# Two of four batches routed inside the attention loop, one dealt there, and other PSUM banks for the shared experts

## The chip, the cores and the metric

The kernel runs on one core of a Trainium2 chip. The core has five engines with a queue each: TensorE (PE, its weight loads shown as PEld), VectorE (DVE), ScalarE (ACT), GpSimd (POOL) and SyncE (SP). An engine works its queue in order; a wait for a semaphore holds everything that stands behind it. SP and POOL also issue DMA transfers. The metric is the time of one execution in microseconds (us) on the device.

## The reference

Four batches of 256 rows with 256 columns go through gated cross attention with 32 heads, and then through a mixture of experts: two shared experts for all rows, and the best 6 of 32 routed experts for each row.

```python
x = x + tanh(g_xattn[0]) * xattn(layernorm(x), ctx, pos, pos, Wq, Wkv, Wout, bout)
flat = layernorm(x).reshape(-1, 256)                 # 1024 tokens
shared = sum(relu(flat @ sw1 + sb1) @ sw2 + sb2 for 2 shared experts) / 2
probs = softmax(flat @ router_w + router_b)          # 32 experts
topk_p, topk_i = top_k(probs, 6); gates = topk_p / sum(topk_p)
routed = sum(gates[:, e] * (relu(flat @ rw1[e] + rb1[e]) @ rw2[e] + rb2[e]) for e in topk_i)
x = x + tanh(g_ffn[0]) * (shared + routed)
```

## The kernel before

The order of the work is written out by hand, engine by engine; semaphores tie the queues together. A tile is 128 rows, a batch `b` has two tiles (`TB`), and there are `NT` = 8 tiles. The program has four stages.

**Projections and rotations** of all batches come first.

**Attention** runs over 32 steps `i` (`GROUPS`; 8 of them, `NG`, to a batch), each with four heads. In step `i` PE transposes queries and keys of step `i+2` into `T_BANK` (`transposes`), makes scores (`score`), waits for DVE's row maxima (`row_max`, L821), which POOL writes beside the queries (`maxima`, L414 and L416), makes shifted scores of earlier steps (`shifted_score`), and multiplies weights by values (`values`). ACT makes the exponentials (L549) and empties `T_BANK` (L506). In odd steps DVE also divides a finished pair of groups (`normalise`, L832 and L837). When a batch is done, its rows are transposed and projected in the same loop: `attention_transposed` at the end of steps 13, 21 and 29, and one tile's `output_projection` (L1286) at the end of steps 15, 17, 23, 25 and 31, all into `T_BANK`. The PE's next `transposes` waits until ACT or DVE (`residual`, L848) has read that bank.

**Routing and shared experts** follow the loop. For each batch: normalised rows (`normalised_rows`), their transposes, the router's scores, the best eight (`choose`), gates (`gates`), counts of earlier rows for each expert by matmul (`counts`), and from these the place of each row and choice (`places`, up to `slot`, L957). POOL then deals: 12 indirect DMAs per batch (L462), 48 in all, each sending a tile's rows to their places in `rows_by_block` in HBM. The shared experts (`shared_hidden`, `shared_transposed`, `shared_out`) stand between these steps on PE, tile by tile, in banks 0, 7, 1, 2, 4 and 6.

**Blocks.** SP waits for all 48 deals (`dealt`) and loads blocks of 128 rows (`xs`, L343); for each of 79 blocks PE works one routed expert (L1450 to L1477), and POOL adds the result to a sum in HBM (L470). PE's first block waits for the last `shared_sum` too:

```python
            pe.wait_ge(shared_ok, NT)
            pe.wait_ge(slot_ok, B)
```

Of the kernel before, what the change touches and what calls it, by code (L numbers as in the profile page):

```python
# [21 lines left out]
def gated_cross_attention_moe(  # L22
# [38 lines left out]
    SPARE = 208  # L61
# [4 lines left out]
    with ExitStack() as keep:  # L66
# [36 lines left out]
        ramp_c = sb("ramp_c", [P, NT])  # L103
        ramp_p = sb("ramp_p", [P, 1])
        gfh = sb("gfh", [P, 1])

        top8 = sb("top8", [P, NT, 8])
# [15 lines left out]
        def sa(name, shape, dt=F32):  # L123
# [33 lines left out]
        XROW_AT, XT_AT = TB * D, 3 * H * HR + TB * D  # L157
        xrow = v_flat[:, XROW_AT:XROW_AT + NT * ROW].rearrange("p (n c) -> p n c", c=ROW)
        xT32 = v_flat[:, XT_AT:XT_AT + KD * TOK].rearrange("p (k n) -> p k n", k=KD)
        assert XROW_AT + NT * ROW <= 3 * H * HR and XT_AT + KD * TOK <= 6 * H * HR  # L160
# [17 lines left out]
        lg = sb("lg", [P, NT, NE])  # L178
        chosen = [sb(f"chosen{i}", [P, TB, TOPK, NE], BF16) for i in range(2)]
        steps8 = sb("steps8", [P, NE, NT])  # L180
        placed = sb("placed", [P, TB, TOPK, NE])
# [39 lines left out]
            sem(n) for n in ("dif_ok", "ex_ok", "mask_ok", "masks_ok", "rk_mm", "row_ok", "slot_ok", "dealt"))  # L221
        later_ok, be_mm, be_ok, isbe_ok, b1_mm, b1_ok = (
# [14 lines left out]
        C_PJ = [[T_BANK, T_BANK] for b in range(B - 1)] + [[S_BANK[0], T_BANK]]  # L237
        C_XT, C_LG, C_RK = [banks[1], banks[2], banks[4], T_BANK], banks[3][:, 0:N], O_BANK[:, N:2 * N]
        C_UP, C_BE = O_BANK[:, 0:B * NE], O_BANK[:, P:P + NBP]
        C_B1 = [O_BANK[:, N + c * P:N + c * P + NBP] for c in range(2)]  # L240
        assert B * NE <= P and NT * NE <= N
        SH_BANK, SHT_BANK = [banks[0], banks[7]], banks[1:3]
        SO_BANK = [banks[4][:, 0:D], banks[6][:, 0:D]]
# [4 lines left out]
        PROJ_STEPS = {NG * (b + 1) + 7 + 2 * t: (b, t) for b in range(B - 1) for t in range(TB)}  # L248
# [110 lines left out]
        def _(pool):  # L359
            steps = [0]  # L360

# [57 lines left out]
            def constants(part):  # L419
# [6 lines left out]
                if part == 1:  # L426
                    pool.wait_ge(pv_mm, 2 * NG)
                    pool.iota(xrow[:, :, X_ID].bitcast(U32), pattern=[[P, NT]], base=0, channel_multiplier=1).then_inc(id_ok, 1)
                    pool.iota(ramp_e[:, :], pattern=[[1, NE]], base=0, channel_multiplier=0, allow_small_or_imprecise_dtypes=True)
                    pool.iota(ramp_c[:, :], pattern=[[P, NT]], base=0, channel_multiplier=0, allow_small_or_imprecise_dtypes=True)  # L430
                if part == 2:
                    pool.iota(ramp_b[:, :], pattern=[[1, NBP]], base=0, channel_multiplier=0, allow_small_or_imprecise_dtypes=True)
                    pool.iota(ramp_p[:, :], pattern=[[0, 1]], base=0, channel_multiplier=1,
                              allow_small_or_imprecise_dtypes=True).then_inc(ramps_ok, 1)

            for g in range(GROUPS):
                maxima(g)
# [14 lines left out]
            inverse_root(6, slice(3 * TB, NT))  # L452

            pool.wait_ge(blank_st, 16 * (SUMS + 1))
            pool.wait_ge(id_ok, 1)
            for b in range(B):
                pool.wait_ge(xn2_ok, TB * (b + 1))
                pool.wait_ge(row_ok, b + 1)
                pool.wait_ge(slot_ok, b + 1)
                for n in range(TB * b, TB * b + TB):  # L460
                    for k in range(TOPK):
                        pool.indirect_dma_start(xd, bass.IndirectOffsetOnAxis(ap=slot[:, n, k:k + 1], axis=0),  # L462
# [11 lines left out]
        def _(act):  # L474
# [109 lines left out]
            for i in range(GROUPS):  # L584
                step(i)
# [940 lines left out]
```

## Time and profile before

| | |
|---|---|
| time, median of 3 runs | 404.68 us (401.33 to 408.31) |
| the profiled execution's own time | 402.14 us |
| its span, first to last instruction | 400.4 us |
| TensorE's mean granted clock | 0.934 of full speed |
| PE, PEld busy | 336.3 us (84%), 263.7 us (66%) |
| DVE, ACT, POOL busy | 245.4, 213.8, 214.8 us |

Shares of the whole span are averages over stages with different limits, so the rows further below are of single stages. "Idle before" of an instruction names what ended the wait. The granted clock is 1.00 at 2.4 GHz and 0.50 at 1.2 GHz.

### The profile page before, as it was taken

The page shows a single profiled execution, that of the slowest core. Times are in us where ns is not written, and L with a number is a line of the kernel's source. Part 1 is how long each engine was busy: PE and PEld are TensorE (multiplying, and loading weights), DVE is VectorE, ACT ScalarE, POOL GpSimd, SP SyncE. Part 2 cuts the span into 40 slices and gives each one's busy share as a digit, 9 for nine tenths or more (in the row PEclk, how much of TensorE's full clock was granted, in tenths as well). Part 3 has the DMA queues.
Part 4 walks back from the last instruction along what each step waited for, and adds up shares of the span by engine and source line. Part 5 has one row for each costly group of instructions (what it writes and reads, how often), then busy time and mean ns, then how long its engine had stood idle before and what let it go on. Part 6 is the DMA issues. An engine that isn't in the chain of part 4 may idle for free.

```text
span 400.4 us, 8584 instructions
## 1 busy us (share of the span) xinstructions
PE 336.3 (84%) x2574; PEld 263.7 (66%) x2574; DVE 245.4 (61%) x765; ACT 213.8 (53%) x536; POOL 214.8 (54%) x242
## 2 busy tenths in 40 slices
PE   8789999999999997523667799999999999999900
PEld 5577666666666555422444589998999899989800
DVE  7997788788788868575440145554545454545526
ACT  4795899988988862110203255555555555555400
POOL 8465331101211112677777248788878887888840
PEclk9999999999999999666659999999999999999975
DMA  7799999983032041133333538888888888887589
GB/s 225 215 308 310 307 335 323 342 180 117 2 86 61 2 120 29 70 112 111 112 113 111 163 70 141 141 150 145 146 141 141 146 142 139 146 143 128 68 168 304
DMA packets 63295, 62.20 MB, mean 155 GB/s; under 512 B 6258, under 2 KB 61588, under 8 KB 63252
## 3 DMA queue, kind: packets, MB, share of 16 engines
q1 hardware_dynamic: 48532, 44.60, 38.3%
q0 software_dynamic: 13680, 17.05, 26.6%
q8 instruction: 24, 0.39, 0.4%
q10 hardware_dynamic: 1040, 0.01, 0.1%
q14 instruction: 19, 0.16, 0.1%
HBM read 29.01 MB, written 32.63 MB: 154 GB/s over the span
## 4 chain that ended last, share of the span: by engine, by line
PE 62%; DVE 14%; ACT 11%; DMA 6%; issue 4%; POOL 1%; SPq 0%; POOLq 0%; DVEq 0%; ACTq 0%
PE psum L1477 15%; PE psum L1459 11%; ACT probs L549 5%; PE psum L1186 5%; PE psum L1233 5%; DMA sum<-ob,xs 4%; PE psum L1395 4%; PE psum L1450 4%; PE psum L1468 4%; PE psum L1374 3%; DVE nmax L821 3%; PE psum L1204 2%; PE psum L1286 2%; PE psum L1087 2%; ACT Vx L631 1%
## 5 line engine op out<-in xcount | busy, mean ns | idle before, releaser
L470 POOL DMA_INDIRECT sum<-ob,xs x79 | 123.0, 1557 | 39.4 <-DVE ob L1057 34.5
L821 DVE TENSOR_REDUCE nmax<-psum 128x2 f32<-128x512 f32 x128 | 79.4, 683 | 10.4 <-PE psum L1186 9.7
L1477 PE MATMUL psum<-w,hT 88*128 (+1 forms) x316 | 81.5, 380 | 0.0
L549 ACT ACTIVATE probs<-psum 128x512 f32<-128x512 f32 x128 | 69.5, 597 | 12.5 <-PE psum L1204 11.4
L1057 DVE TENSOR_SCALAR ob<-psum,gate 128x256 f32<-128x256 f32 x79 | 38.2, 484 | 48.2 <-PE psum L1477 46.1
L668 ACT ACTIVATE hT<-psum,b1b 88x128 f32<-88x128 f32 x158 | 48.8, 358 | 35.2 <-PE psum L1468 35.2
L1459 PE MATMUL psum<-w,xT 128*128 x316 | 60.4, 314 | 0.3 <-ACT xT L659 0.3
L1477 PEld LDWEIGHTS psum<-w,hT 88*128 88x128 f32 (+1 forms) x316 | 53.8, 190 | 4.6 <-issue 0.3
L462 POOL DMA_INDIRECT rows_by_block<-Vx,slot x48 | 46.3, 966 | 18.0 <-issue 14.3
L414 POOL CAST Qx<-nmax 128x8 fp32r<-128x8 f32 x32 | 6.3, 197 | 84.0 <-DVE nmax L821 84.0
L659 ACT ACTIVATE xT<-psum 128x256 f32<-128x256 f32 x79 | 30.2, 383 | 38.9 <-PE psum L1450 38.9
L1459 PEld LDWEIGHTS psum<-w,xT 128*128 128x128 f32 x316 | 47.3, 190 | 1.0 <-issue 1.0
L1040 DVE COPY hb<-psum 128x176 f32<-128x176 f32 x79 | 27.0, 342 | 28.5 <-PE psum L1459 28.4
L1186 PE MATMUL psum<-QK 32*128 32x256 f32 x256 | 38.9, 319 | 3.3 <-DVE nmax L821 2.6
L1204 PE MATMUL psum<-QT,QK 32*128 32x256 f32 x256 | 37.7, 327 | 0.9 <-ACT probs L549 0.8
L1186 PEld LDWEIGHTS psum<-QK 32*128 32x128 f32 x256 | 25.8, 183 | 18.2 <-issue 10.5
L1233 PE MATMUL psum<-probs,Vx 128*32 128x256 f32 x512 | 34.3, 385 | 0.0
L1395 PE MATMUL psum<-w2s,Vx 128*128 128x256 f32 (+1 forms) x48 | 16.6, 495 | 19.4 <-ACT Vx L631 19.4
L1450 PE MATMUL psum<-ident,xs 128*128 128x128 f32 x158 | 30.1, 272 | 0.6 <-DVE x_sb L993 0.6
L1468 PE MATMUL psum<-ident,hb 128*88 128x128 f32 x158 | 30.2, 273 | 0.0
L1450 PEld LDWEIGHTS psum<-ident,xs 128*128 128x128 f32 x158 | 22.0, 140 | 8.8 <-DVE x_sb L993 1.0
L1204 PEld LDWEIGHTS psum<-QT,QK 32*128 32x128 f32 x256 | 25.1, 183 | 2.2 <-issue 1.1
(177 smaller groups left out, 476.4 us busy)
## 6 DMA issues: line engine op xcount, KB each, us to landing
rows_by_block<-blank SPq DMA_DIRECT2D x1, 10744.0 KB, 38.2
xs<-rows_by_block SPq DMA_DIRECT2D x79, 136.0 KB, 2.6
w<-in_L_ffn_rw_dram SPq DMA_DIRECT2D x2, 2816.0 KB, 21.3
w<-in_L_ffn_rw_dram SPq DMA_DIRECT2D x16, 352.0 KB
sum<-blank SPq DMA_DIRECT2D x3, 1152.0 KB, 13.5
w<-sum SPq DMA_DIRECT2D x12, 256.0 KB, 5.5
sum<-ob,xs POOLq DMA_INDIRECT x79, 4.0
x_sb<-in_x_dram SPq DMA_DIRECT2D x4, 256.0 KB, 4.0
```

Source lines behind the costliest of these rows:

```text
L462: pool.indirect_dma_start(xd, bass.IndirectOffsetOnAxis(ap=slot[:, n, k:k + 1], axis=0), xrow[:, n, :], None).then_inc(dealt, 16)
L470: pool.indirect_dma_start(yd[i], bass.IndirectOffsetOnAxis(ap=xs[b % ROWS_AHEAD][:, X_ID:X_ID + 1].bitcast(U32), axis=0), ob[i][:, :], Non ...
L549: act.activation(probs[g % 2][:, :, n, :], st_bank(g, n)[:, :].rearrange("p (t q) -> p t q", t=TB), ACT.Exp, scale=SCALE).then_inc(exp_ok, 1)
L668: ins = act.activation(hT[b % 2][0:HC, c, :], HT_BANK[b % 2][0:HC, c * P:(c + 1) * P], ACT.Relu, bias=b1b[0:HC, c, b:b + 1])
L821: dve.tensor_reduce(nmax[i % 2][:, :, n], S_BANK[(4 * i + n) % SB][:, :].rearrange("p (t k) -> p t k", t=TB), AX.X, ALU.max, negate=True). ...
L1186: ins = pe.matmul(S_BANK[(4 * i + n) % SB][:, qt * N:(qt + 1) * N], QK[i % RING][h, 0, qt * P:(qt + 1) * P], QK[i % RING][h, 1, :], start= ...
L1204: ins = pe.matmul(st_bank(i, n)[:, kt * N:(kt + 1) * N], QK[i % RING][h, 1, kt * P:(kt + 1) * P], QT[i % 2][h, :], start=True, stop=True)
L1233: ins = pe.matmul(O_BANK[HR * h:HR * h + HR, 0:N], Vx[:, TB * b + kt, GH * g + h, :], probs[i % 2][:, kt, h, :], start=(kt == 0 and not se ...
L1450: ins = pe.transpose(XT_BANK[b % 2][:, k * P:(k + 1) * P], xs[r][:, k * P:(k + 1) * P], ident[:, :])
L1459: ins = pe.matmul(H_BANK[b % 2][:, 0:HID], xT[b % 3][:, k, :], w1[:, k, bass.ds(expert[b] * HID, HID)], start=(k == 0), stop=(k == KD - 1))
L1468: ins = pe.transpose(HT_BANK[b % 2][0:HC, c * P:(c + 1) * P], hb[b % 2][:, c * HC:(c + 1) * HC], ident[:, :])
L1477: ins = pe.matmul(Y_BANK[b % 2][:, 0:D], hT[b % 2][0:rows, c, :], w2[0:rows, bass.ds(expert[b], 1), c, :].rearrange("p a n -> p (a n)"), s ...
```

## The change

Each step of the routing of batches 0 and 1 (`EARLY` = 2) moves into the attention loop, some steps after what it needs. For batch `b` they are: the inverse root and its refinement on POOL (`scales`, step 8b+16), normalised rows on DVE (8b+18), their transposes on PE (8b+19), the router's scores (8b+20), the choice on DVE and POOL (8b+21 to 8b+23), gates (8b+23). For batch 0 the counts follow (step 24), then the block numbers and places on POOL and DVE (25 to 27), and POOL issues seven of its deals after the maxima of steps 28 to 31. For batch 1 counts and `places` stand after the loop. Transposes, scores and counts use `T_BANK`. Output projections stand one step apart, at 14, 15, 22, 23, 30 and 31, so that the sixth, before behind the loop, is inside. Whole block counts come from rounding three times instead of from 256 comparisons and a sum. The shared experts get banks 2 and 3 (hidden), 4 and 1 (transposed) and 6 and 0 (result), and their first tiles stand ahead of the last batch's projection.

```diff
-        PROJ_STEPS = {NG * (b + 1) + 7 + 2 * t: (b, t) for b in range(B - 1) for t in range(TB)}
+        PROJ_STEPS = {NG * (b + 1) + 6 + t: (b, t) for b in range(B - 1) for t in range(TB)}
+        EARLY = B - 2
+        ROWS_STEPS = {NG * b + 19: b for b in range(EARLY)}
+        SCORE_STEPS = {NG * b + 20: b for b in range(EARLY)}
+        COUNT_STEPS = {24: 0}
...
-        SH_BANK, SHT_BANK = [banks[0], banks[7]], banks[1:3]
-        SO_BANK = [banks[4][:, 0:D], banks[6][:, 0:D]]
+        SH_BANK, SHT_BANK = banks[2:4], [banks[4], banks[1]]
+        SO_BANK = [banks[6][:, 0:D], banks[0][:, 0:D]]
...
+            EACH = TB * TOPK
+            DEALT_AT = {28: (0, 2), 29: (2, 3), 30: (3, 5), 31: (5, 7)}
             for g in range(GROUPS):
                 maxima(g)
...
+                if g in DEALT_AT:
+                    deal(*DEALT_AT[g])
+                for b in range(EARLY):
+                    if g == NG * b + 16:
+                        scales(b)
+                    if g == NG * b + 21:
+                        marks_of(b)
+                if g == 25:
+                    blocks_needed(0)
+                if g == 26:
+                    places_early(0)
+            deal(DEALT_AT[31][1], DEALT_AT[31][1] + 1)
+            inverse_root(EARLY + 4, slice(TB * EARLY, TB * EARLY + TB))
+            deal(DEALT_AT[31][1] + 1, EACH + EACH // 2)
             pool.wait_ge(pv_mm, GROUPS)
...
+            inverse_root(B + 3, slice(NT - TB, NT))
+            deal(EACH + EACH // 2, NT * TOPK)
...
                     pe.wait_ge(t_ok, i)
...
+                if i - AHEAD - 1 in ROWS_STEPS:
+                    pe.wait_ge(x2T_ok, ROWS_STEPS[i - AHEAD - 1] + 1)
+                if i - AHEAD - 1 in SCORE_STEPS:
+                    pe.wait_ge(lg_ok, SCORE_STEPS[i - AHEAD - 1] + 1)
+                if i - AHEAD - 1 in COUNT_STEPS:
+                    pe.wait_ge(rk_ok, COUNT_STEPS[i - AHEAD - 1] + 1)
...
-            second_rows_transposed(0)
+            second_rows_transposed(B - 2)
             outputs(PAIRS - 1)
-            second_rows_transposed(1)
-            router_scores(0)
-            router_scores(1)
+            router_scores(B - 2)
+            shared_hidden(0)
...
             attention_tile_transposed(B - 1, 1).then_inc(aT_mm, 1)
+            shared_hidden(1)
             for t in range(TB):
                 output_projection(B - 1, t)
```

On POOL, before, from the last `maxima` to the first deals (waits in brackets):

```order
L414 CAST Qx<-nmax1 128x2x4 [waits s_max]
L416 TENSOR_TENSOR Qx<-nmax1,Qx 128x2x4 [waits mhi_ok]
L378 TENSOR_TENSOR rough<-veps,halves 128x4 [waits var_ok]
L378 TENSOR_TENSOR rough<-veps,halves 128x2 [waits var_ok]
L448 MEMSET hT0 64x128 [waits root_ok,pv_mm]
L450 MEMSET Vx 32x128 [waits ones_ok]
L448 MEMSET hT1 64x128 [waits ones_ok]
...
L378 TENSOR_TENSOR rough<-veps,halves 128x2 [waits var_ok,ones_ok]
L462 DMA rows_by_block<-Vx,slot 10112x272 [waits row_ok,xn2_ok,slot_ok,id_ok,blank_st]
L462 DMA rows_by_block<-Vx,slot 10112x272 x11
```

And now, from the last `maxima`:

```order
L425 CAST Qx<-nmax1 128x2x4 [waits s_max]
L427 TENSOR_TENSOR Qx<-nmax1,Qx 128x2x4 [waits mhi_ok]
L502 DMA rows_by_block<-Vx,slot 10112x272 x3
L389 TENSOR_TENSOR rough<-veps,halves 128x2 [waits var_ok]
L502 DMA rows_by_block<-Vx,slot 10112x272 x4
L502 DMA rows_by_block<-Vx,slot 10112x272 [waits row_ok,xn2_ok,slot_ok,id_ok,blank_st]
L502 DMA rows_by_block<-Vx,slot 10112x272 x5
L534 MEMSET hT0 64x128 [waits root_ok,pv_mm]
L536 MEMSET Vx 32x128 [waits ones_ok]
...
L389 TENSOR_TENSOR rough<-veps,halves 128x2 [waits var_ok,ones_ok]
L502 DMA rows_by_block<-Vx,slot 10112x272 x6
```

Ahead of the last inverse root, which needs the last batch's variances, 18 deals now stand where none stood; 30 stand behind it.

On DVE, before, step 23 and the start of step 24 (the middle of attention):

```order
L832 RECIPROCAL rden0<-psum 128x16 [waits q2_ok,ot_mm,norm_ok]
L837 TENSOR_TENSOR attn<-psum,rden0 128x2x32 [waits rd_ok]
...
L821 TENSOR_REDUCE nmax1<-psum 128x2 [waits s_mm,m_ok]
L821 TENSOR_REDUCE nmax1<-psum 128x2 [waits s_mm] x3
L848 SCALAR_TENSOR_TENSOR x_sb<-psum,gx,x_sb 128x256 [waits pj_mm]
L821 TENSOR_REDUCE nmax0<-psum 128x2 [waits s_mm,m_ok]
```

And now, step 23 (`mask` and `red` belong to the routing of batch 0):

```order
L917 RECIPROCAL rden0<-psum 128x16 [waits q2_ok,ot_mm,norm_ok]
L922 TENSOR_TENSOR attn<-psum,rden0 128x2x32 [waits rd_ok]
...
L933 SCALAR_TENSOR_TENSOR x_sb<-psum,gx,x_sb 128x256 [waits pj_mm]
L906 TENSOR_REDUCE nmax1<-psum 128x2 [waits s_mm,m_ok]
L971 TENSOR_REDUCE mask<-Vx 128x64
L906 TENSOR_REDUCE nmax1<-psum 128x2 [waits s_mm] x2
L977 TENSOR_REDUCE red<-ex 128x2 [waits ex_ok]
L978 RECIPROCAL red<-red 128x2 [waits dve_step]
L979 SCALAR_TENSOR_TENSOR Vx<-ex,gf,red 128x2x6 [waits dve_step]
...
L813 BN_STATS stats<-x_sb 128x6 [waits pj_ok]
```

The residual that follows the even projection step 22 stands behind `normalise` in an odd step, and the routing's instructions stand among the maxima.

On PE, before, from the transposes of the last batch's attention to the first shared tile:

```order
L1263 MATMUL psum<-ident,attn 128x128 [waits exp_ok,norm0_ok,pj_ok]
...
L1286 MATMUL psum<-wout_sb,Vx 128x256 [waits aT_ok,out_w_ld]
...
L1335 MATMUL psum<-ident,Vx 128x128 [waits xn2_ok]
...
L1344 MATMUL psum<-rtw_sb,Vx 128x32 [waits lg_ok,x2T_ok]
...
L1364 MATMUL psum<-mask,before_ 128x32 [waits ramps_ok,o_ok,mask_ok]
...
L1374 MATMUL psum<-w1s,Vx 128x352 [waits pj_ok,ws_ld]
```

And now, from the end of attention to the last batch's projection:

```order
L1348 MATMUL psum<-probs1,Vx 32x256 x7
L1414 MATMUL psum<-ident,Vx 128x128 [waits masks_ok,xn2_ok]
...
L1359 MATMUL psum<-ident,oT1 128x128 [waits norm_ok,q2_ok,o_ok]
...
L1423 MATMUL psum<-rtw_sb,attn 128x32 [waits x2T_ok]
...
L1504 MATMUL psum<-w1s,attn 128x352 [waits exp_ok,ws_ld]
...
L1378 MATMUL psum<-ident,attn 128x128 [waits norm0_ok,pj_ok]
...
L1378 MATMUL psum<-ident,attn 128x128 [waits norm_ok]
...
L1504 MATMUL psum<-w1s,attn 128x352 x2
L1401 MATMUL psum<-wout_sb,Vx 128x256 [waits aT_ok,out_w_ld]
```

Two tiles of `shared_hidden` have moved ahead of the projection from which the last batch's variances come.

## Rows read from the trace of the kernel before

**Rows 1.** Windows by stage: busy us (instructions) per engine, granted clock, DMA share, GB/s.

```profile
100.00:130.00 30.00, 28.89 (x350) 19.01 (x349) 24.84 (x51) 26.22 (x57) 4.49 (x25) 1.00 0.19 50
...
170.00:176.00 6.00, 0.42 (x10) 0.31 (x8) 5.06 (x24) 0.00 (x0) 4.57 (x5) 0.78 0.31 116
```

**Rows 2.** Timeline, from the first deal to the first block: start, duration.

```profile
162.36 1.24 POOL L462 DMA_INDIRECT rows_by_block<-Vx,slot  x1 [3.67 <-DVE slot L957]
...
222.06 0.96 POOL L462 DMA_INDIRECT rows_by_block<-Vx,slot  x1 [0.30 <-issue]
...
224.50 20.77 SPq L343 DMA_DIRECT2D xs<-rows_by_block  x16
...
229.24 0.66 PE L1450 MATMUL psum<-ident,xs 128*128 128x128 f32 x4 [0.58 <-DVE x_sb L993]
```

**Rows 3.** DMA issues from 160 to 235 us: count, KB each, median us to landing.

```profile
xs<-rows_by_block SPq DMA_DIRECT2D x12, 136.0 KB, 3.0
rows_by_block<-Vx,slot POOLq DMA_INDIRECT x48, 2.4
```

**Rows 4.** Timeline of POOL, `maxima` of steps 10, 12, 13, 15 and 31.

```profile
66.19 0.20 POOL L414 CAST Qx<-nmax 128x8 fp32r<-128x8 f32 x1 [2.40 <-DVE nmax L821]
...
72.60 0.20 POOL L414 CAST Qx<-nmax 128x8 fp32r<-128x8 f32 x1 [2.40 <-DVE nmax L821]
...
76.13 0.20 POOL L414 CAST Qx<-nmax 128x8 fp32r<-128x8 f32 x1 [3.04 <-DVE nmax L821]
...
83.28 0.20 POOL L414 CAST Qx<-nmax 128x8 fp32r<-128x8 f32 x1 [3.17 <-DVE nmax L821]
...
140.28 0.20 POOL L414 CAST Qx<-nmax 128x8 fp32r<-128x8 f32 x1 [2.91 <-DVE nmax L821]
```

**Rows 5.** Timeline of attention, a projection step (23) and an odd step (25).

```profile
111.71 1.13 PE L1286 MATMUL psum<-wout_sb,Vx 128*128 128x256 f32 x4
...
116.38 0.26 DVE L832 RECIPROCAL rden<-psum 128x16 f32<-128x16 f32 x1 [0.18 <-ACT QT L555]
...
116.58 0.36 PE L1167 MATMUL psum<-ident_r,Qx 128*128 128x128 f32 x2
...
116.94 2.47 DVE L821 TENSOR_REDUCE nmax<-psum 128x2 f32<-128x512 f32 x4
...
117.68 0.38 PE L1186 MATMUL psum<-QK 32*128 32x256 f32 x1 [0.17 <-DVE nmax L821]
```

**Rows 6.** Groups of DVE instructions in routing: count, busy us, mean ns.

```profile
L911 DVE TENSOR_REDUCE mask<-chosen 128x64 bf16<-128x384 bf16 x4 | 3.2, 798 | 0.1
...
L908 DVE TENSOR_TENSOR chosen<-ramp_e,Vx 128x384 bf16<-128x384 f32 x4 | 2.3, 575 | 0.1
```

**Rows 7.** Timeline behind attention: roots, projection to variances, one `places`, shared tile 4.

```profile
150.25 0.70 POOL L378 TENSOR_TENSOR rough<-veps,halves 128x2 f32<-128x2 f32 x1 [6.39 <-DVE veps L736]
...
154.30 1.96 PE L1286 MATMUL psum<-wout_sb,Vx 128*128 128x256 f32 x8 [1.49 <-ACT Vx L609]
...
157.69 0.16 DVE L736 TENSOR_TENSOR veps<-mv,consts 128x2 f32<-128x2 f32 x1
...
170.46 0.43 DVE L933 TENSOR_TENSOR steps<-psum,ramp_c 128x256 f32<-128x256 f32 x1 [4.06 <-PE psum L1364]
...
175.07 0.18 DVE L971 TENSOR_TENSOR old_off<-old_off,off_up 128x32 f32<-128x32 f32 x1
...
216.11 1.56 PE L1395 MATMUL psum<-w2s,Vx 128*128 128x256 f32 x6 [0.99 <-ACT Vx L631]
```

**Rows 8.** Windows of 1 us, columns as in rows 1.

```profile
160.00:161.00 1.00, 0.00 (x0) 0.00 (x0) 0.91 (x3) 0.00 (x0) 0.00 (x0) 1.00 0.00 0
163.00:164.00 1.00, 0.58 (x3) 0.58 (x4) 0.97 (x9) 0.00 (x0) 0.70 (x2) 0.58 0.00 0
204.00:205.00 1.00, 0.61 (x4) 0.61 (x4) 0.29 (x2) 0.00 (x0) 0.70 (x2) 0.50 0.37 139
210.00:211.00 1.00, 1.00 (x4) 0.42 (x2) 0.00 (x0) 0.46 (x1) 0.69 (x2) 0.53 0.16 52
```

More of the change, by code:

```diff
@@ L177, in gated_cross_attention_moe @@
         ob = [sb(f"ob{i}", [P, D]) for i in range(SUMS)]
[L178 to L181, printed above, removed]
         upto_j = sb("upto_j", [P, P])
@@ new lines, in deal @@
+            def deal(first, last):
+                for j in range(first, last):
+                    n, k = j // TOPK, j % TOPK
+                    b = n // TB
+                    if k == 0 and n % TB == 0:
+                        pool.wait_ge(blank_st, 16 * (SUMS + 1))
+                        pool.wait_ge(id_ok, 1 + b // 2)
+                        pool.wait_ge(xn2_ok, TB * (b + 1))
+                        pool.wait_ge(row_ok, b + 1)
+                        pool.wait_ge(slot_ok, b + 1)
+                    pool.indirect_dma_start(xd, bass.IndirectOffsetOnAxis(ap=slot[:, n, k:k + 1], axis=0),
+                                            xrow[:, n, :], None).then_inc(dealt, 16)
@@ new lines, in block_ends, with slots, early @@
+            def block_ends(b, had):
+                return dve.tensor_tensor_scan(upto[:, b, :], had, consts[:, 0, 0:NE], upto[:, b - 1, NE - 1:NE] if b else 0.0,
+                                              ALU.add, ALU.add)
+            def slots(b):
+                with nc.allow_low_precision("whole numbers"):
+                    dve.tensor_reduce(slot[:, TB * b:TB * b + TB, :], placed[:, :, :, :], AX.X, ALU.add).then_inc(slot_ok, 1)
+            def early(i, part):
+                for b in range(EARLY):
+                    at = i - NG * b
+                    if (at, part) == (18, 0):
+                        dve.wait_ge(nstep_ok, b + 1)
+                        dve.wait_ge(pv_mm, NG)
+                        normalised_row(TB * b)
+                    if (at, part) == (18, 2):
+                        normalised_row(TB * b + 1)
+                    if (at, part) == (21, 0):
+                        scores(b)
+                    if (at, part) == (21, 1):
+                        then(eight_best(b))
+                    if (at, part) == (21, 2):
+                        where_best(b).then_inc(at8_ok, 1)
+                    if (at, part) == (22, 1):
+                        dve.wait_ge(exp_row_ok, b + 1)
+                        dve.wait_ge(pv_mm, 2 * NG)
+                        then(choice_of(b))
+                    if (at, part) == (23, 0):
+                        mask_of(b)
+                    if (at, part) == (23, 2):
+                        gate_sums(b)
+                if (i, part) == (26, 1):
+                    dve.wait_ge(had_ok, 1)
+                    block_ends(0, blocks[:, 0, :]).then_inc(upto_ok, 1)
+                if (i, part) == (27, 3):
+                    dve.wait_ge(placed_ok, 1)
+                    slots(0)
@@ L1433, in _ @@
             ins.then_inc(b1_mm, 1)
-            for n in range(2, NT):
+            for n in range(4, NT):
                 shared_out(n)
```

443 lines of the change are left out of this document (242 added, 201 removed).

## The prediction, made before the changed kernel had run

> **What bounds the kernel now.** I read the windows by stage first. In attention PE, ACT and DVE are all nearly full (28.89, 26.22 and 24.84 of 30 us) and POOL is nearly idle, 4.49 [rows 1]. Behind it the picture turns: from 170 to 176 us PE works 0.42 of 6 us while DVE (5.06) makes places and POOL (4.57) deals [rows 1]. So the stage between attention and the blocks is a chain, and the timeline tells which one ends last. POOL's 48 deals start at 162.36 and 222.06 us, 59.7 / 47 = 1.27 us apart; SP's loads go out at 224.50; PE's first block starts at 229.24, released by DVE's last shared sum [rows 2]. A deal lands 2.4 us and a block 3.0 us after its issue [rows 3], so the deals alone would have let the blocks start at 224.5 + 3.0 = 227.5. Two limits thus lie 1.7 us apart, the shared experts last and the dealing just behind. Removing work from one alone would give 1.7 us; this change moves both. From the first block to the end nothing is edited: that part keeps its length.
>
> I count from c, the start of the maxima of step 31, which is 140.28 [rows 4]. Before, the first deal is at c+22.1, the last at c+81.8, the first block at c+89.0.
>
> **What the change adds to attention.** A pair of steps in which `T_BANK` does no other work takes 72.60 - 66.19 = 6.41 us; with the attention transposes of step 13 it takes 83.28 - 76.13 = 7.15 [rows 4], so such a use costs 0.74. From step 13 to 31, 18 steps, it is 64.15 us, 6.46 over nine plain pairs, for seven uses: three transposes (2.2) and four projections, 1.06 each, about the 1.13 that PE spends on one [rows 5]. Now the same stretch holds thirteen uses.
> - Transposes of attention, three, 2.2, and of normalised rows, two: the same four transposes and one ACT copy, 1.5.
> - Projections at odd steps, two, 2.1.
> - Projections at even steps, three. The reader, DVE's residual, now stands behind `normalise` in an odd step. There PE's next transposes start at 116.58, but `normalise` ends at 116.94 [rows 5]; a residual behind it would hold PE until about 117.4. The score that follows, at 117.68, waits for the first maximum anyway [rows 5], so I charge 0.55 of these 0.84: 1.6 each, 4.8.
> - Router scores, two, at even steps. Their small matmuls I take at the projection's 1.06. Their reader stands behind the first maximum too (0.62 of L821's 2.47, and 0.2 more): PE is held until 117.8 and the score slips by 0.85 [rows 5]. 1.9 each, 3.8.
> - Counts, one: no row shows them beside attention. Between 0 and the 0.74 of a larger use, 0.4.
>
> Together 14.8, so 8.3 more than now. DVE adds the routing of two batches: the mask 0.80, the choice 0.58 [rows 6], and by the same group view some 2.6 for rows, scores, best eight and gates, 4.0 a batch. Mostly they fill the holes that the bank uses leave; where no use falls (steps 26 and 27 above all) DVE's maxima and `normalise` already fill 5.9 of 6.4. I charge 1.7 there. At step 29 a deal stands ahead of POOL's copy of the choice, for which DVE waits in step 30: 1.0 more. So attention ends **11 us later**. The bounds are 5 (all bank waits and DVE work hidden) and 17 (8.3 and all 8 us of DVE, none hidden).
>
> The other POOL work in attention (refinement, block numbers, places, seven deals) I cost at nothing: POOL has some 2.9 us free in every step, before each of these rows ("2.40", "3.17" [rows 4]), and no step gets more than about 2.8. A step that gets more delays the maxima by the excess.
>
> One rule speaks against dealing here. The deals before ran beside a DVE that worked 5.06 of 6 us, and kept to 1.27 us apart [rows 1, 2]. The Trainium skill (SBUF — State Buffer, "Who interferes with whom") says that DVE instructions with two SBUF inputs, or in a 2-port mode, and GpSimd's exclude each other for a whole instruction. By that each of seven deals could be held for one `chosen`, 0.58 us, 4 us in all and 395 for the sum; the trace shows no such lengthening.
>
> **What it takes out behind attention.** Now POOL, from c: maxima until c+0.5, three deals to c+4.6, an inverse root of 0.70 [rows 7], ten deals to c+18.0, four memsets to c+19.0. Then comes the root of the last batch, for which POOL waits, with 30 deals queued behind it. Before, that batch's projection starts at 154.30, c+14.0, and the variances are done 3.55 us later, c+17.6 [rows 7]. Now two hidden tiles stand ahead of the projection (each at most the 1.56 of a shared result [rows 7]) and one router less (1.0), which gives c+16.1; and `places(1)`, 4.8 us as one now takes [rows 7], stands ahead of the rows that PE transposes first. I walk it to c+16.5; at worst c+19. Variances at c+20.1, root at c+20.8, last of 30 deals at c+20.8+0.3+29 x 1.27 = c+57.9, landed at c+60.3, first block at **c+63.3** (62 to 66) against c+89.0.
>
> The slots are in time for that: batch 1's at c+8.2 for a deal at c+10.3, batch 2's by the same walk at c+27 for c+28, batch 3's at c+35 for c+44.
>
> The shared experts end earlier. Tile 4's result starts at 216.11 and the first block 13.1 us later [rows 2, 7]; by the walk tile 4 comes at c+41, so they would end at c+54, nine before the deals. **Dealing becomes the limit**, and PE idles for nine us. In the trace the granted clock falls from 1.00 to 0.50 after PE has idled from 159.9 to 163.4, and comes back only at 210.5 after it has worked from 204.4 on [rows 8]: 6.1 us at half speed, some 3.3 us of work late with the ramp. I charge the blocks 3.3 (0 to 3.5).
>
> **Sum.** c moves to 151.3, the first block to 214.6, and 3.3 are lost: 229.2 - 214.6 - 3.3 = 11.3 us gained. Against the profiled execution's 402.1 that is 390.8. The runs' median, 404.7, lies 0.6% above this execution, the lowest at 401.3; I take half of that and forecast 392.
>
> **The rivals.**
> - Attention hides nearly all (5 to 7 us longer) and the clock holds: 402.1 - (229.2 - 146.3 - 63.3) = 382.5 to 386. For it: DVE has 5 of 30 us free. Against: T_BANK's uses cost their full PE time today.
> - The shared experts stay last, at half clock. Four tiles take 13.1 us at full clock [rows 2, 7], mostly PE's; at half clock I estimate 7 us a tile, seven tiles from c+22, so that they end near c+71: 402.1 - (229.2 - 222.3) = 395. For it: the stage runs at half clock today [rows 8]. Against: PE's holes in my walk are at most 2 us, and the 3.5 us hole is what dropped it.
> - Attention stretches by 16 to 20: 396 to 400. The uses now stand in rows of six (19 to 24), so that one late reader may push the next.
> - Slower than before, by one mechanism: POOL's early steps hold up the maxima. Nine steps (16, 21, 24 to 26, 28 to 31) give POOL waits or long work ahead of its next `maxima`, on which PE's next scores hang; a deal at step 28 also waits for `slot`. It decides from 11.3 / 9 = 1.3 us a step; at 2.5 a step it is 22 us and the time 413. For it: POOL works in order, and a root of 0.70 for two columns shows that small operations can be dear [rows 7]. Against: the copy beside it takes 0.20 [rows 4].
> - The early deals come to nothing, because `slot` is late and they pile up behind step 31: seven deals, 9 us, and 400.
>
> **How the numbers follow.** Forecast 0.55 (387 to 396); all hidden 0.12; half clock 0.13; longer attention or deals late 0.13; slower 0.07. A change under 2% can hardly be told from none here (the runs spread by 1.7%): faster by more means under 396.6, which takes the first two and half of the third, 0.74; within 2% 0.19; slower 0.07. The range of 383 to 400 leaves out part of the second case below and the last above.
>
> **What would show it.** Maxima of step 31 near 151; a deal of 0.96 every 1.27 us almost without a break from there, with one gap of 1 to 3 us behind the eighteenth; the last near 209; PE idle for some nine us ahead of the first block, which starts near 215, its first blocks at clock 0.50; and the first blocks released by a load, not by DVE. I am wrong if attention grows by over 17 us, if DVE's last shared sum still releases the blocks, or if POOL waits for `slot` between batches.

## The result and the profile after

The changed kernel takes 387.07 us (median of 4 runs, 384.65 to 388.73), the one before 403.39 beside it. The ratio is 0.959, with a 95% interval of 0.954 to 0.964; by the medians it is 16.3 us less. The forecast was 392, with 383 to 400 as its range. The profiled execution took 387.09 us, its span is 385.3.

As in the prediction, c is the start of the maxima of step 31. The timeline of the changed kernel, POOL's `maxima` of steps 13, 28 and 31, answers to [rows 4]:

```profile
76.11 0.20 POOL L425 CAST Qx<-nmax 128x8 fp32r<-128x8 f32 x1 [2.80 <-DVE nmax L906]
...
133.12 0.20 POOL L425 CAST Qx<-nmax 128x8 fp32r<-128x8 f32 x1 [2.77 <-DVE nmax L906]
...
146.72 0.20 POOL L425 CAST Qx<-nmax 128x8 fp32r<-128x8 f32 x1 [1.98 <-DVE nmax L906]
```

Up to step 13 nothing differs (76.11 against 76.13). From there to step 31 attention takes 70.61 us against 64.15, so c comes 6.4 us later; the prediction had 11. Windows by stage answer to [rows 1]:

```profile
100.00:130.00 30.00, 28.15 (x336) 19.09 (x335) 26.86 (x66) 24.88 (x55) 8.37 (x34) 1.00 0.17 50
170.00:176.00 6.00, 5.54 (x31) 4.01 (x29) 5.45 (x26) 1.94 (x6) 4.48 (x6) 1.00 0.27 97
```

In attention DVE goes from 24.84 to 26.86 of 30 us and POOL from 4.49 to 8.37. From 170 to 176 us PE, which worked for 0.42, now works for 5.54: the shared experts run beside the deals.

The same kernel's timeline, from the 18th deal to the first block, answers to [rows 2]:

```profile
163.92 0.97 POOL L502 DMA_INDIRECT rows_by_block<-Vx,slot  x1 [0.30 <-issue]
...
168.44 0.72 POOL L389 TENSOR_TENSOR rough<-veps,halves 128x2 f32<-128x2 f32 x1 [2.53 <-DVE veps L822]
169.36 1.03 POOL L502 DMA_INDIRECT rows_by_block<-Vx,slot  x1 [0.20 <-issue]
...
204.43 0.48 DVE L1113 SCALAR_TENSOR_TENSOR x_sb<-psum,gfh,x_sb 128x256 f32<-128x256 f32 x1 [2.37 <-PE psum L1527]
...
206.41 0.97 POOL L502 DMA_INDIRECT rows_by_block<-Vx,slot  x1 [0.30 <-issue]
...
208.87 3.21 SPq L353 DMA_DIRECT2D xs<-rows_by_block  x7
...
211.13 1.12 PE L1581 MATMUL psum<-ident,xs 128*128 128x128 f32 x4 [6.74 <-DMA xs<-rows_by_block]
```

Behind the 18th deal POOL waits 2.53 us for the last batch's variances. Then 30 deals follow 37.05 / 29 = 1.28 us apart, the last at c+59.7, and the first block starts at c+64.4. It is released by a load, and PE had idled for 6.74 us: the deals end last, no longer DVE's shared sum. The first block starts 18.1 us earlier than before.

From the first block to the end of the span it is 385.3 - 211.1 = 174.2 us, against 400.4 - 229.2 = 171.2 before, 3.0 longer. The clock was low at the start of the blocks. Windows of 1 us, the granted clock third from the right, answer to [rows 8]:

```profile
157.00:158.00 1.00, 0.74 (x4) 0.53 (x4) 0.41 (x3) 0.60 (x1) 0.77 (x1) 0.86 0.86 276
158.00:159.00 1.00, 1.00 (x7) 1.00 (x6) 0.20 (x2) 0.00 (x0) 0.69 (x2) 0.50 0.80 278
...
164.00:165.00 1.00, 1.00 (x4) 0.64 (x3) 0.00 (x0) 0.00 (x0) 0.96 (x2) 0.73 0.38 139
...
205.00:206.00 1.00, 0.00 (x0) 0.00 (x0) 0.00 (x0) 0.00 (x0) 0.86 (x1) 0.75 0.37 139
...
215.00:216.00 1.00, 1.00 (x7) 0.89 (x6) 0.27 (x2) 0.00 (x0) 0.00 (x0) 0.63 0.85 262
216.00:217.00 1.00, 1.00 (x9) 0.96 (x8) 0.36 (x4) 0.89 (x3) 0.00 (x0) 1.00 0.14 47
```

The granted clock is at 0.50 (1.2 GHz) from 158 to 164 us, again from 189 to 195, and from 206 on, while PE idles, until it has worked for four us at the blocks. 18.1 - 3.0 = 15.1 us is the difference of the two spans.

The first of these falls matters too. The timeline of PE there:

```profile
153.21 1.07 PE L1348 MATMUL psum<-probs,Vx 128*32 128x256 f32 x16 [0.61 <-ACT probs L625]
156.33 0.65 PE L1414 MATMUL psum<-ident,Vx 128*128 128x128 f32 x4 [2.05 <-DVE Vx L851]
...
159.39 2.69 PE L1504 MATMUL psum<-w1s,attn 128*128 128x352 f32 x4
...
162.73 2.25 PE L1504 MATMUL psum<-w1s,attn 128*128 128x352 f32 x4
164.82 1.89 PE L1401 MATMUL psum<-wout_sb,Vx 128*128 128x256 f32 x8
...
169.40 1.35 PE L1504 MATMUL psum<-w1s,attn 128*128 128x352 f32 x4
```

Behind a hole of 2.05 us the two hidden tiles of the shared experts take 2.69 and 2.25 us where a later one takes 1.35, and the last batch's projection, on whose variances POOL waits, stands behind them.

### The profile page after: what moved, and what is told of

It is laid out like the page before. It is cut to its first block, busy times and chain, and to the rows that moved or that the text cites. A ratio compares the mean times of both kernels' runs of the same rounds, so it can differ in the third digit from the quotient of the medians.

```text
span 385.3 us, 8620 instructions
## 1 busy us (share of the span) xinstructions
PE 333.4 (87%) x2574; PEld 262.3 (68%) x2574; DVE 240.6 (62%) x753; ACT 214.6 (56%) x537; POOL 221.7 (58%) x267
## 4 chain that ended last, share of the span: by engine, by line
PE 55%; DVE 12%; issue 10%; POOL 9%; DMA 8%; ACT 5%; SPq 0%; POOLq 0%; DVEq 0%
PE psum L1608 14%; PE psum L1590 10%; POOL rows_by_block L502 7%; PE psum L1301 6%; PE psum L1348 5%; DVE nmax L906 5%; DMA sum<-ob,xs 5%; PE psum L1581 4%; PE psum L1599 3%; ACT probs L625 2%; PE psum L1319 2%; PE psum L1196 2%; PE psum L1282 2%; PE psum L1401 2%; POOL sum L546 2%
## 5 line engine op out<-in xcount | busy, mean ns | idle before, releaser
L906 DVE TENSOR_REDUCE nmax<-psum 128x2 f32<-128x512 f32 x128 | 80.9, 683 | 13.2 <-PE psum L1301 12.3
L1590 PE MATMUL psum<-w,xT 128*128 x316 | 61.6, 318 | 0.3 <-ACT xT L746 0.3
L1608 PEld LDWEIGHTS psum<-w,hT 88*128 88x128 f32 (+1 forms) x316 | 53.8, 190 | 4.6 <-issue 0.3
L502 POOL DMA_INDIRECT rows_by_block<-Vx,slot x48 | 47.6, 991 | 14.4 <-issue 14.1
L1590 PEld LDWEIGHTS psum<-w,xT 128*128 128x128 f32 x316 | 48.3, 193 | 0.9 <-issue 0.9
L582 ACT ACTIVATE QK<-psum 128x512 fp32r<-128x512 f32 x32 | 19.5, 610 | 5.0 <-PE psum L1282 5.0
```

Source lines behind the costliest of these rows:

```text
L906: dve.tensor_reduce(nmax[i % 2][:, :, n], S_BANK[(4 * i + n) % SB][:, :].rearrange("p (t k) -> p t k", t=TB), AX.X, ALU.max, negate=True). ...
L1590: ins = pe.matmul(H_BANK[b % 2][:, 0:HID], xT[b % 3][:, k, :], w1[:, k, bass.ds(expert[b] * HID, HID)], start=(k == 0), stop=(k == KD - 1))
L1608: ins = pe.matmul(Y_BANK[b % 2][:, 0:D], hT[b % 2][0:rows, c, :], w2[0:rows, bass.ds(expert[b], 1), c, :].rearrange("p a n -> p (a n)"), s ...
```

## The experiments

Theory D: POOL's dealing is the limit, so that the first block follows the last deal by 4.7 us, and whatever shortens the queue of deals, or POOL's wait in it, shortens the whole. Rival S: the shared experts, or PE's clock, set the first block. Times of profiled runs are told from c or from the first block on, since the start, and attention as will be seen, differ by some 2 us from one execution to the next. Ratios are to the kernel before on the same chip.

**Deals behind attention.** Only the early dealing is undone:

```diff
-            DEALT_AT = {28: (0, 2), 29: (2, 3), 30: (3, 5), 31: (5, 7)}
...
-                if g in DEALT_AT:
-                    deal(*DEALT_AT[g])
...
-            deal(DEALT_AT[31][1], DEALT_AT[31][1] + 1)
+            deal(0, 8)
...
-            deal(DEALT_AT[31][1] + 1, EACH + EACH // 2)
+            deal(8, EACH + EACH // 2)
```

> All twelve deals of batch 0 stand behind attention; everything else as in the changed kernel. Theory D (the dealing on POOL is the limit, with the 2.5 us for which POOL waits behind the 18th deal as its only slack): five deals started before the maxima of step 31, so 5 x 1.28 = 6.4 us of dealing come behind, the wait of 2.5 absorbs its part, and the first block starts 3.9 us later (2.9 if step 30 no longer waits for POOL's copy of the choice): 390 to 391 against 387.1. If every deal counted in full: 393.5. Rival S (the shared experts or PE's clock set the first block): the first block does not move, 387.

Measured: 391.61 us, ratio 0.972 (0.967 to 0.977). The last deal is at c+64.0 and the first block at c+68.7, 4.3 us later than with early deals; POOL's wait shrinks from 2.53 to 0.54 (6.4 - 2.0 = 4.4). That is D's number, and not all five deals in full. Steps 28 to 31 take 148.59 - 134.97 = 13.62 us without any deal and 146.72 - 133.12 = 13.60 with them: the deals in attention cost nothing there, the one ahead of POOL's copy of the choice included.

**Blocks kept warm.** `keep_warm(n, bank)` is a helper of the kernel: PE multiplies the identity n times into a bank that is free and waits for the last. The profile lists two instructions for each.

```diff
+            pe.wait_ge(b1_ok, 1)
+            keep_warm(36, O_BANK)
             pe.wait_ge(shared_ok, NT)
```

> 36 small matmuls of the identity, into a free bank, fill the 6.7 us for which PE waits ahead of the first block; the rest is unchanged. If the 3.0 us by which the blocks take longer than before come from the low clock at their start: the granted clock stays up, the first block still starts near 211, and the span from there to the end is 171.2 as in the kernel before: 384.1. Rival (the blocks start slowly because their rows, loads and copies come late, whatever the clock): 387.

Measured: 384.26 us, ratio 0.953 (0.950 to 0.956). Timeline and a window of this kernel:

```profile
203.67 8.20 PE L1196 MATMUL psum<-ident 128*128 128x128 f32 x72
212.62 0.41 PE L1581 MATMUL psum<-ident,xs 128*128 128x128 f32 x2 [0.75 <-DMA xs<-rows_by_block]
...
362.91 2.08 PE L1608 MATMUL psum<-w,hT 88*128 x8
```

```profile
212.00:213.00 1.00, 0.38 (x2) 0.20 (x2) 0.00 (x0) 0.00 (x0) 0.00 (x0) 1.00 0.94 283
```

The first block is again at c+64.4 (c is 148.2 here) and again released by a load, but the clock is at 1.00, and from there to the end it is 384.1 - 212.6 = 171.5 us. Of the 3.0 us 2.7 are gone, but only half of that in the blocks. Their last matmuls, in the kernel before and in the changed kernel:

```profile
379.17 2.09 PE L1477 MATMUL psum<-w,hT 88*128 x8
```

```profile
362.80 2.08 PE L1608 MATMUL psum<-w,hT 88*128 x8
```

From the first block to the end of these it is 152.0 us before, 153.75 in the changed kernel and 152.4 with the blocks kept warm: 1.4 us gone with the low clock. Behind them, where the sum is read back and the result stored, it is 19.1, 20.4 and 19.1 us. That part takes 18.8 to 20.4 in all the profiles, without regard to the clock ahead of the blocks.

**The root two deals later, and the hidden tiles behind the projection.** Two ways to take away POOL's wait; in the second, ScalarE's reading of the first tile (`shared_rows`) moves with it:

```diff
-            deal(DEALT_AT[31][1] + 1, EACH + EACH // 2)
+            deal(DEALT_AT[31][1] + 1, EACH + EACH // 2 + 2)
...
-            deal(EACH + EACH // 2, NT * TOPK)
+            deal(EACH + EACH // 2 + 2, NT * TOPK)
```

> POOL's root of the last batch's variances stands behind the 20th deal in place of the 18th, so that two deals are made while POOL would wait. Theory D: the last deal and the first block come 2.5 us earlier, 384.6. Rival S (shared experts, whose last sum is done at 204.9, or PE's clock set the first block): no change, 387. If the later root makes the last batch's slots late, POOL waits ahead of the 37th deal and the gain goes.

```diff
...
-            shared_rows(0)
             for t in range(TB):
                 last_transposed_attention(t)
+            shared_rows(0)
...
-            shared_hidden(0)
             pe.wait_ge(pj_ok, TB * (B - 1))
...
-            shared_hidden(1)
             for t in range(TB):
                 output_projection(B - 1, t)
+            shared_hidden(0)
+            shared_hidden(1)
```

> The first two hidden tiles of the shared experts (2.69 and 2.25 us on PE at granted clock 0.50) stand behind the output projection of the last batch in place of ahead of it. Theory D: the variances come some 4 us earlier, POOL's wait of 2.5 us goes and no more than that, since POOL deals until 165.9 anyway: first block 2.5 us earlier, 384.6; the shared experts end up to 2 us later, still ahead of it. Rival C (the low clock merely moves: PE idles where the tiles stood and projects at half speed): variances where they were, 387. Rival S: 387 to 389, with the shared experts.

Measured: 385.61 us, ratio 0.959 (0.956 to 0.962), for the root; 382.84, 0.953 (0.949 to 0.957), for the tiles. The timelines of POOL, first with the later root, then with the tiles behind:

```profile
147.98 0.20 POOL L425 CAST Qx<-nmax 128x8 fp32r<-128x8 f32 x1 [1.94 <-DVE nmax L906]
...
169.47 0.72 POOL L389 TENSOR_TENSOR rough<-veps,halves 128x2 f32<-128x2 f32 x1
...
176.37 0.97 POOL L502 DMA_INDIRECT rows_by_block<-Vx,slot  x1 [1.10 <-DVE slot L989]
...
205.86 0.97 POOL L502 DMA_INDIRECT rows_by_block<-Vx,slot  x1 [0.30 <-issue]
```

```profile
146.66 0.20 POOL L425 CAST Qx<-nmax 128x8 fp32r<-128x8 f32 x1 [1.99 <-DVE nmax L906]
...
166.06 0.72 POOL L389 TENSOR_TENSOR rough<-veps,halves 128x2 f32<-128x2 f32 x1 [0.21 <-DVE veps L822]
...
204.03 0.97 POOL L502 DMA_INDIRECT rows_by_block<-Vx,slot  x1 [0.30 <-issue]
```

With the later root the wait is gone, but the deals now run ahead of batch 2's slots and 1.10 us of waiting comes back at the 25th (0.30 lie between any two deals): last deal at c+57.9, 1.8 us earlier in place of 2.5, and the ratio shows nothing of it. With the tiles behind, the wait is 0.21, the last deal at c+57.4, the first block at c+62.1: 2.3 us of the 2.5. The clock fell there all the same (0.50 from 158 to 164; the projection took 3.75 us), so the gain came from the order alone. In both the first block follows the last deal by 4.7 to 4.8 us, as D has it. The second kernel's span is 4.3 us shorter than the changed kernel's; what this has beyond the earlier first block lies behind that block, most of it (1.2) behind PE's last matmul.

**The hole filled.** The same wait attacked through the clock:

```diff
+            keep_warm(8, S_BANK[1])
             second_rows_transposed(B - 2)
```

> Eight small matmuls of the identity (0.23 us each) fill PE's idle 2.05 us at 154.3, behind attention's last values; the rest is the changed kernel. If that hole is what the fall of the granted clock to 0.50 from 158 to 164 follows: the clock stays at 1.00 there, the two hidden tiles take 1.35 us each in place of 2.69 and 2.25, the last batch's variances come 3 us earlier, POOL's wait of 2.5 us goes: 384.6. Rival (the clock falls anyway, since the work before and behind the hole is sparse too): 387.

Measured: 384.54 us, ratio 0.953 (0.950 to 0.957). Timeline of PE, and the eight us in one window:

```profile
155.06 2.05 PE L1196 MATMUL psum<-ident 128*128 128x128 f32 x16
157.21 0.63 PE L1414 MATMUL psum<-ident,Vx 128*128 128x128 f32 x4
...
159.44 1.43 PE L1504 MATMUL psum<-w1s,attn 128*128 128x352 f32 x4
...
161.14 1.35 PE L1504 MATMUL psum<-w1s,attn 128*128 128x352 f32 x4
162.33 1.89 PE L1401 MATMUL psum<-wout_sb,Vx 128*128 128x256 f32 x8
```

```profile
157.00:165.00 8.00, 7.36 (x46) 5.57 (x45) 5.36 (x23) 2.17 (x6) 6.17 (x7) 1.00 0.54 192
```

The clock stays up, the tiles take 1.43 and 1.35, the variances are there at c+18.2 in place of c+21.6, POOL's wait is gone, and the first block starts at c+61.6, 2.8 us earlier. So the fall followed this hole of two us.

**Without the last batch's deals.** This kernel leaves out twelve deals and SP's wait for them; what the routed experts add to the last batch is then missing.

```diff
-            sp.wait_ge(dealt, 16 * NT * TOPK)
+            sp.wait_ge(dealt, 16 * 3 * TB * TOPK)
...
-            deal(EACH + EACH // 2, NT * TOPK)
+            deal(EACH + EACH // 2, 3 * EACH)
```

> The twelve deals of the last batch are left out, and with them the routed experts' share of that batch's tokens; their places in the blocks hold blank rows, and all blocks run. Theory D: the last deal comes 12 x 1.276 = 15.3 us earlier, at 191 and landed by 196, before the shared experts end at 204.9. So the next limit shows: VectorE's last shared sum releases the first block at about 205.5, PE does not idle ahead of it and the clock stays up: 5.6 + 3.0 us less, 378.5. If something else holds the blocks behind the deals, less.

Measured: 376.94 us, ratio 0.935. The last deal is at 189.38, and the timeline shows what comes next:

```profile
199.88 0.48 DVE L1113 SCALAR_TENSOR_TENSOR x_sb<-psum,gfh,x_sb 128x256 f32<-128x256 f32 x1 [2.37 <-PE psum L1527]
...
200.42 0.66 PE L1581 MATMUL psum<-ident,xs 128*128 128x128 f32 x4 [0.58 <-DVE x_sb L1113]
```

The shared sum releases the first block again, as before the change. That this is c+53.8 and not c+58.8 was not expected: in this execution the clock stayed at 1.00 from 162 on, where the changed kernel's fell to 0.50 from 189 to 195. Why it held, no run here tells; it need not be this kernel's doing, since two of its four executions took 374.5 and 375.8 us at a mean granted clock of 0.973 and 0.974, the other two 378.1 and 379.1 at 0.962 and 0.960.

**What attention was charged with.** Two kernels test the prices of the prediction's sum. In one the readers of `T_BANK` stand ahead, in the other VectorE has more to do:

```diff
-                    if (at, part) == (21, 0):
-                        scores(b)
...
+                if i - 1 in PROJ_STEPS:
+                    residual(*PROJ_STEPS[i - 1])
                 if i >= 7 and i % 2:
                     normalise((i - 7) // 2)
-                if i - 1 in PROJ_STEPS:
-                    residual(*PROJ_STEPS[i - 1])
+                if i - 1 in SCORE_STEPS:
+                    scores(SCORE_STEPS[i - 1])
```

> In attention VectorE reads the output projection ahead of normalise in place of behind it, and the router scores ahead of a step's maxima in place of behind the first. By the prediction's prices (an even projection costs 1.6 against 1.06 for an odd one, and a router score 0.62 of its 1.9, because these readers stand behind other work) the maxima of step 31 come 3 x 0.55 + 2 x 0.62 = 2.9 us earlier than 146.7, and the whole falls by as much: 384. Rival: those waits were hidden by other waits of PE, or normalise and the maxima now come late instead: step 31 within 1 us of where it was or later, 387 to 388.

```diff
+                if i in (25, 26, 27) and part == 2:
+                    with nc.allow_low_precision("zeros and ones"):
+                        dve.tensor_reduce(extra[:, :, :], chosen[0][:, :, :, :].rearrange("p t k e -> p t e k"), AX.X, ALU.add)
```

> VectorE makes batch 0's mask once more (0.80 us, into a tile that nobody reads) in each of the steps 25, 26 and 27, where T_BANK has one use in three steps. By the prediction (VectorE is full where no bank use leaves holes, so that its work counts in full there) attention grows by 3 x 0.8 = 2.4 us: 389.5. Rival (VectorE has slack there that added work fills): by less than 0.8 us, 387 to 388.

Measured: 386.37 us, ratio 0.956 (0.952 to 0.960), and 390.23, 0.965 (0.960 to 0.970). With the readers ahead, steps 13 to 31 take 148.91 - 78.07 = 70.84 us, against 70.61: in sum nothing is gained. Its `maxima` of steps 20 to 23 show that two effects cancel:

```profile
104.05 0.20 POOL L425 CAST Qx<-nmax 128x8 fp32r<-128x8 f32 x1 [2.99 <-DVE nmax L906]
...
108.86 0.20 POOL L425 CAST Qx<-nmax 128x8 fp32r<-128x8 f32 x1 [4.24 <-DVE nmax L906]
...
112.54 0.20 POOL L425 CAST Qx<-nmax 128x8 fp32r<-128x8 f32 x1 [2.89 <-DVE nmax L906]
...
117.89 0.20 POOL L425 CAST Qx<-nmax 128x8 fp32r<-128x8 f32 x1 [4.86 <-DVE nmax L906]
```

Steps 20 and 21 take 8.49 us against 110.76 - 101.78 = 8.98 in the changed kernel: PE's wait of 0.84 us for VectorE's read of the scores is gone. Step 22, at whose end the projection stands that is now read ahead of `normalise`, takes 5.35 against 115.66 - 110.76 = 4.90. Steps 28 and 29 are 0.16 shorter in the same way, and steps 14 and 30 are 0.47 and 0.12 longer. With three masks more, steps 24 to 29 take 20.14 us against 18.90: 1.24 of the added 2.4 count, between the two theories. From step 0 to 31 its profile shows 117.3 us against 113.1; the other 3.0 are the clock, which fell twice there, at 105 and at 139 us.

That fall had not been seen in the kernel before, and the changed kernel's own profile has none. But of the twelve profiles of it and the variants told of so far and below, the last kernel left out, five show one, in the step behind the router scores (21 or 29), and that step takes 1.4 to 1.6 us longer. Windows of the kernel with warm blocks:

```profile
104.00:105.00 1.00, 0.62 (x6) 0.62 (x6) 1.00 (x5) 0.81 (x3) 0.00 (x0) 0.88 0.00 0
105.00:106.00 1.00, 1.00 (x12) 0.69 (x14) 0.97 (x7) 0.57 (x2) 0.00 (x0) 0.50 0.06 16
```

**The edits together.** Tiles behind the projection and 36 small matmuls; the same with the hole filled and 26 matmuls; with one more early deal; and with the wait for the router scores filled too:

```diff
-            DEALT_AT = {28: (0, 2), 29: (2, 3), 30: (3, 5), 31: (5, 7)}
+            DEALT_AT = {28: (0, 2), 29: (2, 3), 30: (3, 6), 31: (6, 8)}
...
                 if i - AHEAD - 1 in SCORE_STEPS:
+                    pe.wait_ge(q2_ok, i - AHEAD - 1)
+                    pe.wait_ge(norm_ok, (i - AHEAD - 5) // 2)
+                    keep_warm(4, T2_BANK)
                     pe.wait_ge(lg_ok, SCORE_STEPS[i - AHEAD - 1] + 1)
```

> The two hidden tiles behind the last projection and the 36 small matmuls ahead of the first block, together. If both act apart from each other, their gains add: 2.3 us of earlier dealing and 2.7 of blocks at full clock, 387.1 - 5.0 = 382, or 380 by the medians. Rival: with the clock raised ahead of the blocks the deals or loads do not come earlier, and one of the gains is lost, 383 to 384.

> Hidden tiles behind the last projection, the hole at 154 filled by eight small matmuls, and 26 small matmuls (5.9 us by the 8.2 us that 36 took) ahead of the first block, so that they end before its rows are there. If the 36 were too many when the deals end early, and this is why the two edits together gave no more than the first alone: first block near c + 62, the blocks in 171.5: 379 to 380. Rival (raising the clock ahead of the blocks costs what it gives once the deals end earlier): 383 to 385.

> As the kernel with all three edits, and one more deal of batch 0 in step 30 of attention, ahead of the maxima of step 31 (POOL idles 1.98 us there). Theory D: one deal less behind attention, the first block 1.28 us earlier, 378 to 379; the same as its neighbour if POOL then waits longer for the last batch's variances, and slower by 1 if the deal delays the maxima.

> As the kernel with the three edits and one more early deal, and four small matmuls more in each of steps 21 and 29, where PE otherwise waits 0.84 us for VectorE's read of the router scores. In five of twelve profiles the granted clock fell to 0.50 for three to four us behind that wait in one of these steps, and attention took 1.5 us longer. If the fall follows that hole: attention stays at 113.1 us from the maxima of step 0 to those of step 31 in every profile, and the median falls below 382.9, to 381 to 382, with a smaller spread. Rival (the fall comes without regard to the hole): median and spread as without it, and a fall may show again; the wait of the four matmuls for each other may add 0.2 us a step.

Measured: 384.84 us (0.952), 383.38 (0.950), 382.87 (0.952, interval 0.946 to 0.959) and 382.42 (0.946, 0.943 to 0.949). The first missed: its 36 matmuls ended at 211.28, when the rows had been there (last deal at 205.14, and 4.7 more makes 209.9), so they held the block for 1.5 us. With 26 the blocks take 381.6 - 209.9 = 171.7 us from c+61.8, as expected, but the median stays 3.4 above the expected 380. Of that the profile shows 1.5, the fall at 105 inside attention; the rest is open. One more early deal brings the last deal from c+57.0 to c+55.6 and the first block to c+60.4. The timeline of PE in that kernel:

```profile
199.10 5.97 PE L1196 MATMUL psum<-ident 128*128 128x128 f32 x52
207.15 0.87 PE L1582 MATMUL psum<-ident,xs 128*128 128x128 f32 x4 [2.08 <-DMA xs<-rows_by_block]
```

Its profiled execution is the shortest of those with all deals, 378.3 us of span. The fourth is the best by its ratio, 1.4% below the changed kernel; its interval overlaps those of the three others. All four medians lie above what was expected, the second within its rival's 383 to 385 although its blocks were as short as forecast, and the first three ratios are not clear of that of the tiles alone (0.953). That the gains add is seen in c and the first block of the profiles, not in the times. The fourth's profile has no fall in attention, but attention takes 0.6 us longer, 113.7 from step 0 to 31 against 113.1; as seven of the twelve profiles had no fall either, this one does not show that the filled wait prevents it.

## Why the prediction was right, point by point

- **The dealing becomes the limit**: right, and shown from both sides: five deals more behind attention, one less, or no wait of POOL move the first block as much as the last deal, and without twelve deals the shared sum takes over. No run undoes the early routing, the places of the shared experts or their banks by themselves, so the 18.1 us are not divided between these parts of the change.
- **Attention, 11 us later**: the step whose size was off, by 4.6 us; that each use of `T_BANK` lengthens attention held. By the rows, thirteen uses and VectorE's work came to 70.61 - 9 x 6.41 = 12.9 us, where the prediction had 14.8 + 1.7 + 1.0 = 17.5. Of the parts, the 1.0 at step 30 is nothing (13.62 against 13.60 us). Of the 1.24 for the places of the scores' readers about half came back: with these ahead, steps 20, 21, 28 and 29 are 0.65 shorter together. The 0.55 for each residual behind `normalise` can't be had back, since with the residual ahead steps 14, 22 and 30 are 1.04 longer; what its old place costs, no run shows. In the 1.7 for VectorE's filled steps, half of added work counted, and the prediction took VectorE for fuller than it was: the two divisions of `normalise` take 0.35 us together, so that a plain pair holds 5.5 of 6.4 us and not 5.9. How the rest of the 4.6 splits is open. The price that the rows of before gave without any refinement, 6.46 / 7 = 0.92 a use, makes 5.5 for six more uses, nearer to the 6.4 than 11 is.
- **POOL's early steps cost nothing**: right for the deals, which were taken out. The refinement and the places were not, and the timeline shows one delay: in step 26 the places keep POOL from 126.87 to 129.79, 2.9 us against the 2.8 allowed, and the `maxima` of step 27 start at 129.86 without any idle time, though VectorE's were done at 129.24. Whether these some 0.5 us lengthened attention, no run shows. Ahead of the `maxima` behind its other early steps POOL idled for 0.89 us or more.
- **The rule against dealing here**: the Trainium skill (SBUF — State Buffer, "Who interferes with whom") says that a VectorE instruction with two SBUF inputs and a GpSimd instruction that reads SBUF exclude each other. The trace agrees in part, where the prediction had read the trace of before against it: none of the 48 deals there was issued while `chosen` or `placed`, the two longest of these instructions in the routing, ran, so it could show nothing. In the changed kernel two deals behind attention were, one of them beside `chosen` (its marks now lie in `Vx`):

```profile
160.94 0.56 DVE L966 TENSOR_TENSOR Vx<-ramp_e,Vx 128x384 bf16<-128x384 f32 x1
161.05 1.29 POOL L502 DMA_INDIRECT rows_by_block<-Vx,slot  x1 [0.30 <-issue]
```

It took 1.29 us, the other 1.12, in place of 0.97. Three deals of this kernel, during which such an instruction began, kept their 0.97, as at 175.80, and the instruction its 0.56. In the profiles of the changed kernel and its variants all 17 deals that were issued with 0.26 us or more of one left took 1.10 to 1.32. The price is far below the 4 us feared: no deal inside attention met one, and POOL's wait behind the 18th took up the two.
- **Variances at c+20.1**: they came at c+21.6, because the hidden tiles, charged 1.56 each at most, took 2.69 and 2.25 at the low clock. The prediction held that holes of two us do not lower the clock, since the fall it had seen stood behind one of 3.5; the filled hole shows that one of 2.05 did. POOL was free at c+19.2, as walked (c+19.0), so the whole 1.5 us went into its wait, which was 2.5 us in place of 1.1, in the upper part of 1 to 3.
- **First block at c+63.3**: c+64.4. The late variances make 1.5 us of it and the deals at 1.28 in place of 1.27 another 0.2; the way from the last deal to the block was 4.7 in place of 5.4. That only 1.1 is left is two errors of opposite sign.
- **Shared experts at c+54**: c+58.2 with the second fall of the clock, c+53.7 in the run in which it held. Since they end before the deals either way, this cost nothing.
- **Blocks lose 3.3**: the mechanism was right, the size was not, and that 3.0 came out is luck. Up to PE's last matmul the blocks lost 1.7 (153.75 against 152.0), of which 1.4 went with the low clock in the run that keeps PE at work; the other 1.3 lie behind it, in a part that varies by 1.6 from profile to profile. In the seven profiles with a low clock at their start the blocks take 153.1 to 154.2 us, in the seven without 152.0 to 152.4, but for one with 153.5. And the clock of before did not stay down until 210.5, as the prediction read it. It was back at 1.00 in between, as in these windows of it:

```profile
170.00:171.00 1.00, 0.42 (x10) 0.31 (x8) 0.51 (x2) 0.00 (x0) 0.79 (x1) 1.00 0.37 139
184.00:185.00 1.00, 0.00 (x0) 0.00 (x0) 0.93 (x3) 0.00 (x0) 0.89 (x1) 1.00 0.43 139
```

The 6.1 us at half speed from 204.4 on, from which the 3.3 came, stand.

The sum had 25.7 us off behind attention, 11 on in it and 3.3 on at the blocks, 11.3 gained; it came out as 24.5, 6.4 and 3.0, 15.1 by the spans. Most of the error is one term's. Of the rivals, the one in which attention hides nearly all (382.5 to 386) was the nearest: attention did take 6.4, but the clock did not hold. "Half clock" was half right: the clock did fall and made the variances late, but the shared experts were not last. "Slower" fell with the deals, which held up no maxima; the places did once, by some 0.5.

## What to carry to other kernels

When a chain behind a dense stage is moved into it, price the uses of the shared resource by what its present uses cost in the rows, all in. Waits of readers added one by one made the price too high here, and a reader moved ahead made the work behind it late. Where a queue of fixed-length transfers ends last, look for the one wait inside it and move what it waits for; each microsecond there was one of the whole until the next wait. An engine that a new limit leaves idle may then work at a lower clock: small matmuls that end just before its input arrives gave back 1.4 us here, and too many cost 1.5.

## What the runs showed of the hardware

- The granted clock fell to 0.50 in or behind a hole of only 2.05 us at the end of attention, in each of the nine profiles of kernels that left it open (with the deals behind attention it is 6.28), and in none of the four that filled it. Inside attention it fell behind a wait of 0.84 us for the read of the router scores, in five of the eleven profiles that have this wait; what decides is not known from these runs.
- Thirty indirect DMAs of 128 rows kept 1.28 us apart, 0.97 on GpSimd and 0.30 to the next, with VectorE 5.45 of 6 us busy beside them and with it idle, at either level of TensorE's clock.
- An indirect DMA issued by GpSimd while VectorE works a 128x384 instruction with two SBUF inputs takes longer: 1.12 us with 0.28 of that instruction left, 1.29 with 0.45, against 0.97. Three that were already being issued when such an instruction began kept 0.97.
